# Semaphores from two sides, one clear per stage: a nine-stage transformer kernel on one core

## What is computed

```python
x = x + L0_xattn(layernorm(x), ctx, mask)   # 16 heads of 128, 257 keys
x = x + L0_attn(layernorm(x))               # 16 heads of 16, 32 tokens
x = x + L0_ffn(layernorm(x))                # 64 experts, 8 per token
x = x + L1_xattn(layernorm(x), ctx, mask)   # RMS norms on q and k
x = x + L1_attn(layernorm(x))               # weights as 4-bit codes and scales
x = x + L1_ffn(layernorm(x))                # 8 experts, 2 per token
```

## Time and profile before

| | us |
|---|---|
| median of 3 runs | 2687.45 |
| lowest and highest run | 2682.81, 2689.44 |
| span of the profiled execution | 2711.5 |
| TensorE busy in it | 2552.4 (94%) |
| VectorE, ScalarE, GpSimd busy | 1351.5, 1271.0, 769.8 |
| mean granted TensorE clock | 0.973 of full speed |

### The profile page before, as it was taken

One profiled execution on the slowest core, in us unless ns is written; L12 is line 12 of the kernel. 1 busy time (PEld: TensorE's weight loads), 2 busy tenths in 40 slices (PEclk: granted clock), 3 DMA queues, 4 the chain that ended last, 5 costly groups with the idle time before them and its releaser, 6 DMA issues. The chain is left out here.

```text
span 2711.5 us, 56681 instructions
## 1 busy us (share of the span) xinstructions
PE 2552.4 (94%) x16582; PEld 1911.9 (71%) x16582; DVE 1351.5 (50%) x4801; ACT 1271.0 (47%) x5190; POOL 769.8 (28%) x979
## 2 busy tenths in 40 slices
PE   6999999989999989997899999999969999999888
PEld 5888888878544434444567877777758888888767
DVE  3555555546577744443444544444424444444434
ACT  2555555544466656664366555566512222222142
POOL 1323323237355520003232333331051111111122
PEclk8999999999899989998899999999989999999999
DMA  5322222110510014422354443332370000000033
GB/s 179 79 62 63 67 65 67 52 41 0 164 47 2 1 56 131 128 68 58 86 142 125 110 109 95 104 109 71 128 180 31 8 6 6 8 8 8 8 87 123
DMA packets 176277, 195.19 MB, mean 72 GB/s; under 512 B 39993, under 2 KB 141687, under 8 KB 175378
## 3 DMA queue, kind: packets, MB, share of 16 engines
q1 hardware_dynamic: 146146, 157.65, 19.8%
q0 software_dynamic: 17744, 32.60, 4.9%
q10 hardware_dynamic: 12256, 3.44, 0.8%
HBM read 150.44 MB, written 56.62 MB: 76 GB/s over the span
## 5 line engine op out<-in xcount | busy, mean ns | idle before, releaser
L2284 PE MATMUL sa_work_ps<-sa_xnT,all_big 128*128 128x128 f32 x2048 | 245.2, 282 | 17.6 <-POOL all_big L2619 6.8
L231 PE MATMUL rt_kn_key_ps<-moe_w_wk,all_big 128*128 128x512 f32 x560 | 253.9, 605 | 7.1 <-remote 4.2
L2284 PEld LDWEIGHTS sa_work_ps<-sa_xnT,all_big 128*128 128x128 f32 x2048 | 240.2, 198 | 21.2 <-POOL all_big L2619 7.1
L718 ACT ACTIVATE xa_probsT<-xa_probsT_ps 128x256 f32<-128x256 f32 x512 | 191.4, 374 | 98.5 <-PE xa_probsT_ps L583 93.0
L563 PE MATMUL xa_misc_ps<-xa_xnT,cross_folded 128*128 128x256 f32 x1024 | 233.2, 382 | 0.7 <-ACT xa_xnT L684 0.7
L606 PE MATMUL xa_misc_ps<-cross_folded,xa_mixT 128*128 128x256 f32 x1024 | 229.3, 379 | 0.0
L563 PEld LDWEIGHTS xa_misc_ps<-xa_xnT,cross_folded 128*128 128x128 f32 x1024 | 196.2, 192 | 31.8 <-ACT xa_misc_ps L693 3.3
L2377 ACT ACTIVATE sa_kT<-sa_work_ps,sa_bias_k 128x128 f32<-128x128 f32 x256 | 73.2, 368 | 303.1 <-PE sa_work_ps L2284 303.1
L606 PEld LDWEIGHTS xa_misc_ps<-cross_folded,xa_mixT 128*128 128x128 f32 x1024 | 194.6, 190 | 26.5
L583 PE MATMUL xa_probsT_ps<-all_ident,xa_probs 128*128 128x128 f32 x1024 | 197.1, 274 | 4.8 <-DVE xa_probs L844 3.6
L231 PEld LDWEIGHTS rt_kn_key_ps<-moe_w_wk,all_big 128*128 128x128 f32 x560 | 104.8, 193 | 130.8 <-issue 109.5
(11 more groups left out here) (395 smaller groups left out, 5049.8 us busy)
## 6 DMA issues: line engine op xcount, KB each, us to landing
all_big<-rk SPq DMA_DIRECT2D x256, 128.5 KB
xa_pair<-pairs SPq DMA_DIRECT2D x64, 256.5 KB, 14.1
pairs<-all_big SPq DMA_DIRECT2D x64, 128.5 KB, 2.9
moe_w_wk<-in_ctx_dram SPq DMA_DIRECT2D x64, 128.0 KB, 2.5
pairs<-xa_keys SPq DMA_DIRECT2D x64, 128.0 KB
cross_folded<-in_L_ffn_w_gate_dram SPq DMA_DIRECT2D x32, 192.0 KB, 2.5
cross_folded<-in_L_ffn_w_up_dram SPq DMA_DIRECT2D x32, 192.0 KB, 2.7
ff_rows<-pairs SPq DMA_DIRECT2D x35, 128.0 KB, 2.0
```

The source lines that it names most:

```text
L231: pe.matmul(self.key_ps[m % self.banks][0:n, :], self.ctxT[:, c * P:c * P + n], self.wk[:, q * 512:(q + 1) * 512], start=True, stop=True). ...
L718: act.activation(probsT[:, b % 2, :, r * P:(r + 1) * P], probsT_ps[s % 2][:, 0:KB * P].rearrange("p (k n) -> p k n", k=KB), ACT.Copy).then ...
L2284: ins = pe.matmul(ps[:, j, :], w[:, c, h * HD:(h + 1) * HD], xnT[:, c, :], start=(c == 0), stop=(c == NC - 1))
```

## The change

Two things change together.

A new object `SIDES` deals out semaphore numbers. All 157 free ones are counted: the 16 lowest are kept for the semaphores that GpSimd's DMAs raise, each used once and never cleared again; the other 141 are a row that odd stages take from the low end and even stages from the high end. A stage and its neighbour thus never share a number.

The clearing block in front of each stage is gone. Instead each stage's SyncE stream begins with one instruction, `clear_next`, which clears in one range everything of the row that the stage itself doesn't use: the numbers that the stage before it left, and all that the next one will take. Nobody waits for it but SyncE's own later instructions. One block remains at the very start of the program, in which SyncE clears all 157 numbers in one instruction.

```diff
+class Sides:
+    ALIKE = 16
+    def start(self, nc):
+        free = sorted(nc.free_semaphores)
+        self.kept, self.first, self.stop = free[:self.ALIKE], free[self.ALIKE], free[-1] + 1
...
+    def take(self):
+        if self.stage % 2:
+            self.lowest += 1
+            return self.lowest - 1
+        self.highest -= 1
+        return self.highest
...
+    def other(self):
+        return range(self.lowest, self.stop) if self.stage % 2 else range(self.first, self.highest)
...
     def block(self):
-        with self.nc.Block() as block:
-            @block.sync
-            def _(sp):
-                for handle in self.sems:
-                    sp.sem_clear(handle)
         return self.ctx.enter_context(self.nc.Block())
+    def clear_next(self, sp):
+        sp.sem_clear(SIDES.other())
...
         @block.sync
         def _(sp):
+            sc.clear_next(sp)
             for q in range(QUARTERS):
...
 def build(nc, I, out):
+    SIDES.start(nc)
+    with nc.Block() as block:
+        @block.sync
+        def _(sp):
+            sp.sem_clear(range(SIDES.kept[0], SIDES.stop))
```

More of the change, by code:

```diff
@@ L64, in apart, with next_stage, take_kept @@
     eng.sem_inc(passed, 1)
+class Sides:
[3 more added lines that the diff above has]
+        self.kept, self.first, self.stop = free[:self.ALIKE], free[self.ALIKE], free[-1] + 1
+        assert free == list(range(free[0], self.stop))
+        self.stage, self.lowest, self.highest = 0, self.first, self.stop
+    def next_stage(self):
+        self.stage += 1
+        if self.stage % 2:
+            self.lowest = self.first
+        else:
+            self.highest = self.stop
+    def take(self):
+        if self.stage % 2:
+            self.lowest += 1
+            return self.lowest - 1
+        self.highest -= 1
+        return self.highest
+    def take_kept(self):
+        return self.kept.pop(0)
+    def other(self):
+        return range(self.lowest, self.stop) if self.stage % 2 else range(self.first, self.highest)
+SIDES = Sides()
 class Scope:
     def __init__(self, nc, ctx, name):
-        self.nc, self.ctx, self.name, self.sems = nc, ctx, name, []
+        self.nc, self.ctx, self.name, self.began = nc, ctx, name, False
     def sb(self, name, shape, dt=F32):
@@ L79, in sem @@
     def sem(self, name):
-        handle = self.ctx.enter_context(self.nc.semaphore(f"{self.name}_{name}"))
-        self.sems.append(handle)
-        return handle
+        if not self.began:
+            SIDES.next_stage()
+            self.began = True
+        return self.ctx.enter_context(self.nc.semaphore(f"{self.name}_{name}", num=SIDES.take()))
     def pool_dma_sem(self, name):
-        self.sems.append(self.nc.alloc_semaphore(name=f"{self.name}_{name}"))
-        return self.sems[-1]
+        return self.nc.alloc_semaphore(name=f"{self.name}_{name}", num=SIDES.take_kept())
     def block(self):
-        with self.nc.Block() as block:
-            @block.sync
-            def _(sp):
-                for handle in self.sems:
-                    sp.sem_clear(handle)
         return self.ctx.enter_context(self.nc.Block())
+    def clear_next(self, sp):
+        sp.sem_clear(SIDES.other())
 def begin(nc, I, x_sb, ident, folded):
```

## The result

The changed kernel takes 2664.32 us (median of 4 runs, 2660.07 to 2667.95) against 2686.34 us (median of 4, 2682.81 to 2689.44) before: a ratio of 0.9919, with an interval from 0.9905 to 0.9933. That is 22.0 us less, where 2660 us had been forecast from a median of 2687.45, 27 us less. The number lies in the range and is almost exactly that of rival A (2664.8 us: the clears and barriers pay in full, the clock pays nothing).

The account below looks back on a forecast made before the run. The kernel was taken as one path of nine stages closed by all-engine barriers, with clears exposed between them. 22.9 us for clears and barriers plus 5 for the clock, 27.9, gave 2660 us; 8-in-10 range 2650 to 2678.

Parts of the forecast that it names:

- rival A: At the stage starts the clock gives nothing back, only clears and barriers pay: 2664.8 us; chance 0.16.
- the forecast's own range: Likeliest case, chance 0.58: from 2654 us, clock kept in all three stages, to 2668 us, no clock gain.
- Clears and barriers (22.9 us): Between stages: clears of eight blocks 20.5 us, eight barriers 2.0, first block net 0.5, less 0.06 for new clears.
- The lower end: Price of a range clear in the new clears: that of a one-number clear, 0.06 us, whatever the range.
- the upper end: Each number in a range costs 58 ns: 22.6 us for 389 numbers in initial block, in and ex.
- Rivals C and E: Range clears cost per number: C, 2671 to 2682.6 us, chance 0.12; E, 93 ns each, 2696 us or more, 0.02.
- Which stages feel SyncE's stream: Of the clears heading each stage's SyncE stream, only those in in and ex delay the path; 0.06 us lost.
- Rival D: At stage boundaries, the wait at L91 hid code fetch or loads, then waited for instead: 2680 to 2687 us; chance 0.06.
- The clock (5 us): Shorter TensorE idles keep its clock at starts of sa0, br, xa1: 3.3 us plus half of 3.1 and 1.4.
- the even chance: At the starts of br and xa1, 1.6 us of idle might keep the clock; half their gain counted.
- The quarter that I let br give back: At br's start, a quarter of TensorE's 5.56 busy us regained by a kept clock: 1.4 us.
- a fall "at a worse moment": Where clock falls remain they may come at a worse moment; the clock term was rounded from 5.6 to 5 us.

Follow-up runs that it names:

- one_clear: Kernel before with its clearing blocks and second barriers kept, each block's single clears joined into one to four range clears; 0.9934 of the kernel before.
- single_clears: Changed kernel with the range clear at the head of each stage's SyncE stream written as one clear per number; 2673.44 us, 0.9976 of the kernel before.
- clock_back: Changed kernel with clearing blocks of single clears put back ahead of sa0 and xa1 alone; 0.9942 of the kernel before.
- before_warm_four: Kernel before with TensorE transposing the identity in the clearing blocks ahead of sa0, ex, br and xa1 alone; 2721.94 us, 0.9989 of the kernel before.
- before_warm: Kernel before with TensorE transposing the identity in every clearing block except that of in; 0.9996 of the kernel before.
- rep_after: Changed kernel, unchanged, profiled and timed again on one chip with a copy of the kernel before; 2698.84 us, 0.9913.
- warm_pe: Changed kernel with extra TensorE transposes of the identity at the starts of xa0, ex and ff1 and in sa1; 0.9905 of the kernel before.
- barrier_back: Changed kernel with an empty block, a barrier and nothing else, ahead of each of the nine stages' blocks; 0.9911 of the kernel before.
- warm_again: The same kernel as warm_pe, run again beside the changed kernel's third execution on one chip; 2656.43 us, 0.99 of the kernel before.
- block_sa0: Changed kernel with the clearing block of 30 single clears put back ahead of sa0 alone; 2660.72 us, 0.9906 of the kernel before.
- after_third: Changed kernel, unchanged, executed a third time on another chip; 2657.56 us against 2682.26, 0.9909 of the kernel before.

## Why the prediction was nearly right, and what it mis-sized

The time came inside the range, but the forecast's own range, 2654 to 2668 us, had been drawn to hold a kernel without any help from the clock. So the number alone doesn't bear the forecast's mechanism out: what came is rival A, to which 0.16 had been given, and that the two lie 5 us apart is why the forecast looks nearly right.

**Clears and barriers (22.9 us).** Right, and shown. The time between stages went from 24.72 to 1.35 us in both pairs, 23.4 us. The two terms inside it were the sizes they should be: one_clear took 20.1 us with the clears alone (20.5 forecast, plus 0.5 at the first block), and a barrier costs 0.33 us, so eight give 2.6 rather than 2.0. The step that mattered was to price a clear by the distance between starts, 58 ns; by the recorded 25 ns the sum would have been 12 us short.

**The price of a range.** The lower end was taken and something near the lower end is what came: 0.15 to 0.29 us on the record and 0.19 to 0.34 us of SyncE's time, instead of 0.06 us each. For the 389 numbers on the path the part that grows is 389 x 1.76 = 0.7 us, not the 22.6 of the upper end. Rivals C and E fall with the first rows, and single_clears shows what C's mechanism does when it is made to happen: two waits for loads, 8.6 and 6.2 us longer.

**Which stages feel SyncE's stream.** Only in and ex, shown by the same run, to within the 1 us by which other stages scatter.

**Rival D, something covered by the wait at L91.** Did not happen: TensorE's first matmul in sa0 comes 0.79 us after its last of xa0, with the stage's barrier as what ended the idle. The idle times were forecast at 0.9, 1.6, 1.6, 3.6 and 5.6 us for sa0, br, xa1, ex and sa1; they are 0.79, 1.55, 1.18, 3.93 and 5.58.

**The clock (5 us).** This is the term that was mis-sized. The three ratios of the changed kernel are 0.9919, 0.9913 and 0.9909, on the mean 0.9914: 23.1 us of 2686, and the time between stages is 23.4 of them. By the three differences of medians (22.0, 27.0 and 24.7) it is 24.6 us. What is left for the clock is between nothing and 1 us, where 5 had been counted; with intervals of 0.0014 to 0.0022 on each ratio, about 2 to 3 us on their mean, I can't say more. The runs that move the clock by other means agree with that but don't narrow it: clock_back leaves 0.4 us (5 either way), before_warm_four 1 to 3 (4 either way), and before_warm, the unclean one, 6 (3 either way). So 5 us lies outside what the changed kernel's own ratios allow, while a term of 2 or 3 us stays possible.

The start of sa0 was sized well. The 36th matmul after sa0's release ends at 10.39 and 10.28 us in the two profiles of before and at 7.23 us in all three of the changed kernel: 3.1 us against 3.3 forecast. In xa1 the clock did fall in all three, behind 1.18 us of idle; that was the even chance. In two it fell with the first matmul, for 6.8 us; in rep_after 2.2 us behind the first matmul, for 3.4 us, as this window shows:

```profile
1309.90:1316.90 7.00, 6.20 (x13) 2.83 (x14) 0.00 (x0) 1.92 (x10) 4.54 (x6) 0.76 0.59 134
```

In warm_pe, which changes nothing in br or xa1, the same place with 1.19 us of idle kept its clock for the whole window:

```profile
1272.40:1279.40 7.00, 6.22 (x17) 2.99 (x18) 0.00 (x0) 3.13 (x18) 4.58 (x6) 1.00 0.57 125
```

The length of the last idle doesn't settle it. In br the clock was kept at the start and the 20th matmul ended at 6.16 us in place of 8.95 and 7.65, but the stage ended no earlier: on one chip it is 86.91 and 87.24 us. The quarter that I let br give back was a guess; near the end of br TensorE waits 3.07 us for VectorE's `br_wT`, in rep_after as in the changed kernel's first profile, so a start that is sooner need not end sooner.

Where did sa0's 3.1 us go? In these pairs of profiles they were there within sa0 and more: the whole stage is 6 us shorter (126.78 to 120.52 on one chip, 126.42 to 120.53 on another). That it is 6 and not 3 is in part luck. With the same start, the 36th matmul ending at 7.23 us, sa0 took 122.67 us in barrier_back, 124.36 in warm_again, 126.55 in single_clears and 127.65 in warm_pe, and roughly with it goes the time that TensorE spends at half clock in the stage: 4 to 7 us in the three changed profiles, 13.1, 9.5, 16.8 and 17.4 us in these four, and 20 to 22 us where the start is slow. So a kept start can be lost again to later falls in its own stage. Against the gain stand a fall that now reaches further into rt (the 10th matmul ends 7.39, 6.17 and 7.09 us after rt's release in the three, 5.85 and 6.03 in the two of before), falls at new places in xa1 (the changed kernel's first profile has four of them behind xa1's start, and xa1 is there 9.5 us longer than in before, but not in the other two), and sa1, which is 2 us longer in the changed kernel. The forecast looked at three starts and held everything else still, with the last half microsecond of rounding for a fall "at a worse moment". That was the mistake, as far as it is known: only the difference between what the starts regain and what the rest loses reaches the end. The difference is measured, at about nothing; where the regained time went is read from single profiles, in which a stage of the same instructions scatters by as much as the term, and isn't shown. That single profiles show up to 10 us less in the stages and the medians do not is the same scatter, seen from the other side.

The Trainium skill (TensorE: Matmul & The Clock Gate, section HAM oscillation), by which the clock comes down only after a long enough idle, would have made the term 7.8 us. The trace disagrees at xa1, where in two of three profiles 1.18 us of idle, the longest in the 5 us before, were followed by 0.51 and 0.52 of full speed for 7 us.

**What stays open.** sa1 takes 605.6 to 606.9 us in the profiles of before, of before with transposes, and of the two kernels with sa0's block back, and 608.0 to 609.9 in those of the changed kernel, one_clear, barrier_back, single_clears and the two kept-busy ones. Neither the length of the idle ahead of it (5.59 us in block_sa0, 5.59 in after_third) nor the numbers of the semaphores (the same in those two) tells them apart. Of all but before and the changed kernel I have one profile each, and no cause.

## What to carry to other kernels

Price instructions of a queue by the distance between their starts, not by their recorded durations (25 against 58 ns for a single clear, 294 against 339 ns for the longest range clear), and look first at what stands where every engine waits: 373 clears of 25 ns were 21 us of this kernel. Before comparing two profiles stage by stage, run both kernels on one chip; a stage that the change does not touch and that moves by 20 us is a sign that they were not. Count a regained clock only as a difference over the whole kernel: a start that is 3 us faster is not 3 us at the end until the falls behind it have been looked at, in more than one execution.

## What the runs showed of the hardware that I had not expected

- A range clear is recorded with about 18 ns and 1.76 ns for each number: 73 ns for 30, 146 for 73, 294 for 157. To SyncE's next instruction it takes some 41 to 45 ns more.
- A barrier of all engines with nothing in it took 0.33 us in eight places of nine, and 0.77 us in the ninth, where one engine's drain came late.
- rt took 263 to 265 us and br 66 to 67 us on two chips (seven profiles), rt 284 to 288 and br 87 to 89 us on two others (five profiles), with the same instructions in these stages but for SyncE's clears. The first profile of before has a third pair, 274 and 86 us, so the two don't always go together. Why was not tried.
- A clock fall behind 1.18 us of idle at xa1's start in each of three profiles, at once in two and 2.2 us later in the third, none there in warm_pe with 1.19 us, and none behind 1.55 us at br's start in the same three.
- Half-clock time taken away by a change bought little: it fell from 142 us to 98 between the copies of one chip, to 58 and 51 with TensorE kept busy, and the last step bought nothing that the medians show. Among the executions of one kernel the two do go together: in the 17 timed runs of before beside the two copies, the 6 with a mean clock of 0.976 or more have spans of 2719 us on the mean, the 8 with 0.972 or 0.973 spans of 2727 us, 8 us longer with some 23 us more at half clock. Which causes which isn't shown.
